# Moving scaled norms, an up projection and an out projection at the end of windowed attention

## The chip, the cores and the metric

The kernel runs on one core of a Trainium2 chip. The core has five engines that run their own instruction streams and meet at semaphores: TensorE (PE, matmuls and transposes; its weight loads are listed as PEld), VectorE (DVE), ScalarE (ACT), GpSimd (POOL) and SyncE (SP, which issues DMAs). The metric is the device time of one execution in microseconds; three executions before the change gave 2340.21, 2340.26 and 2348.76, median 2340.26.

## The reference

Input x is 4 batches of 1024 tokens by 256 features. First comes causal attention with 16 heads of 16, which this change does not touch. Then a stack of two layers of windowed attention and feed-forward; B, N there are 4 and 1024, 8 heads of 64, windows of 128, HID = 682:

```python
def _layer(x, wqkv, qs, ksc, wo, lg, lb, w1, b1, w2, b2):
    h = shift_token(x)                    # second half of the features from the token before
    q, k, v = split(h @ wqkv); q, k = l2norm(q) * qs, l2norm(k) * ksc
    q, k = rotary_xpos(q, k)
    o = local_attention(q, k, v)          # each window sees itself and the one before
    x = x + o @ wo
    h = shift_token(x)
    h = (h - mean) / sqrt(var + 1e-05) * lg + lb
    a, g = split(h @ w1 + b1)
    return x + (a * gelu(g)) @ w2 + b2
```

The result is x + stack(layernorm(x)), after the first attention's residual.

## The kernel before

`layers` does the two layers, four batches each: eight passes of attention(it) and feed_forward(it), written out one after the other in each engine's stream. What stands in a stream is done in that order; an instruction starts when those ahead of it on its engine are through and its semaphores have the values it waits for. `Count.of(it, i)` is the value after item i of pass it (negative i: items of the pass before).

Attention goes through 32 units (UNITS), each a couple of heads of one window of 128 tokens, four units a window. For unit u PE makes scores into one of the score banks s0 and s1 (L1382, two units at a time), DVE masks them and takes the maximum (L1894), ACT takes the exponential (L1628), PE turns the probabilities in pt_ps (L1448, two units behind), ACT copies them out (L1644), and PE multiplies by the values into o_ps (L1473). For each window the sums of probabilities are inverted, widened by ACT (L1653), spread over the features by PE in turn_ps (L1457); ACT copies o_ps to o_t (L1660) and DVE scales o_t (L1951). When the last units are in work, no new scores follow, and this chain over PE, ACT and DVE has little beside it.

The out projection (L1395) works on halves of 512 tokens: half c, feature block m. The half c = 0 and its norm are done inside attention, beside later windows: out projection, residual sum (DVE, L1904), turn to tokens first (PE, L1403), statistics and normalising (DVE, L1913, L1924), turn back (PE, L1412), scaled norms (`scale_norm`, ACT, L1636: four ACTIVATEs, a full and a rounded copy of two feature blocks) and the low part (`split_norm`, DVE, L1930). scale_norm stands at unit NORM_AT + 6 = 30 of ACT's loop, split_norm at NORM_AT + 7 of DVE's. These steps use two of the three banks of qkv_ps, as ln_ps.

The feed-forward has six up projections (L1435) for each half, each of 12 matmuls into a couple of banks (the last, of 42 features, 6 matmuls into one bank): s0 and s1, or pt_ps and o_ps, in turn (`up_pair`). Behind each: GELU (ACT, L1691), gate product (DVE, L1986, counts hidden_ready), rounding (ACT, L1699), low part (DVE, L1992, counts hidden_split). Up projection i waits for the gate product of i - 2, which frees its banks. The down projection (L1516, 18 matmuls for each feature block) follows, and the next pass's query, key and value projections (L1336) stand between. The first up projection is in the attention loop, at u = UNITS; the out projection of the second half follows it. At the end of the feed-forward the next pass's first scores (L1382) go into s0 and s1.

A float32 matmul (not a transpose, nor one of the rounded float32r kind) appears in the traces as two records, so the out projection's 8 matmuls are "x16" there.

Of the kernel before, what the change touches and what calls it, by code (L numbers as in the profile page):

```python
# [22 lines left out]
P = 128  # L23
# [1061 lines left out]
def layers(nc, ident, neg_half, passed, a):  # L1085
# [5 lines left out]
    with ExitStack() as ctx:  # L1091
# [11 lines left out]
        up_pair = lambda c, j: pair[(c + j) % 2]  # L1103
# [213 lines left out]
        def _(pe):  # L1317
# [48 lines left out]
            def scores(it, g):  # L1366
                w = 2 * g // PAIRS
                pe.wait_ge(turn_copied.sem, turn_copied.of(it, 2 * w + 1))
                pe.wait_ge(s_masked.sem, s_masked.of(it, 4 * g - 1))
                if g == 0:  # L1370
                    pe.wait_ge(hidden_ready.sem, hidden_ready.of(it, -1))
                first, last = max(0, w - 1), w
                if first % KR < last % KR:
                    runs = [(first, last + 1)]
                else:
                    runs = [(t, t + 1) for t in range(first, last + 1)]
                for h, (t0, t1) in itertools.product(range(2), runs):
                    for u in (2 * g, 2 * g + 1):
                        p, side = place(u, h)
                        r = slice(side * HD2, (side + 1) * HD2)  # L1380
                        to = (h + 1) * PW - (w + 1 - t0) * P
                        mm = pe.matmul(s_ps[side][:, to:to + (t1 - t0) * P], q_t[r, w % 2, p, :],  # L1382
                                       k_t[r, p, t0 % KR * P:(t0 % KR + t1 - t0) * P], start=True, stop=True)
                        if h and t1 == w + 1:
                            mm.then_inc(s_ready.sem, 1)

            def project_out(it, c, m):
# [3 lines left out]
                if c == 1 and m == 0:  # L1391
                    pe.wait_ge(hn_t_ready.sem, hn_t_ready.of(it, KD - 1))
                pe.wait_ge(o_scaled.sem, o_scaled.of(it, (c + 1) * WPC - 1))
                for k in range(INNER // P):
                    mm = pe.matmul(ln_ps[m], w_out[:, k, m * P:(m + 1) * P],  # L1395
                                   o_t[:, k, :], start=k == 0, stop=k == INNER // P - 1)
                mm.then_inc(wo_ready.sem, 1)

            def tokens_first(it, c):
                pe.wait_ge(mid_ready.sem, mid_ready.of(it, (c + 1) * KD - 1))  # L1400
                for t in range(TC):
# [14 lines left out]
            def up(it, c, j):  # L1416
                i = c * HT + j
                pe.wait_ge(hn_t_split.sem, hn_t_split.of(it, (c + 1) * KD - 1))
                if i == 0:
                    pe.wait_ge(s_masked.sem, s_masked.of(it, 2 * UNITS - 1))  # L1420
                elif i == 1:
                    pe.wait_ge(pt_copied.sem, pt_copied.of(it, UNITS - 1))
                    pe.wait_ge(o_copied.sem, o_copied.of(it, NT - 1))
                elif i == HT:
                    pe.wait_ge(hidden_ready.sem, hidden_ready.of(it, i - 1))
                elif i == HT + 1:
                    pe.wait_ge(out_ready.sem, out_ready.of(it, KD - 1))
                elif i > 1:
                    pe.wait_ge(hidden_ready.sem, hidden_ready.of(it, i - 2))
# [9 lines left out]
            def attention(it):  # L1439
# [39 lines left out]
                for u in range(UNITS + 3):  # L1479
# [22 lines left out]
                    if u == UNITS:  # L1502
                        up(it, 0, 0)
# [3 lines left out]
            def feed_forward(it, more):  # L1507
                def down(c, m):
# [3 lines left out]
                    for n, (j, w, h) in enumerate(steps):  # L1512
# [3 lines left out]
                        mm = pe.matmul(pair[c][m][:, :], w_down(w, j, m)[0:rows], hidden[0:rows, h, j, :],  # L1516
# [16 lines left out]
                up(it, 0, 1)  # L1533
                tokens_first(it, 1)
                for j in range(2, HT):
# [46 lines left out]
        def _(act):  # L1582
# [56 lines left out]
            def attention(it):  # L1639
# [23 lines left out]
                for u in range(UNITS + 3):  # L1663
# [17 lines left out]
                    if u == NORM_AT + 6:  # L1681
                        scale_norm(it, 0)
# [160 lines left out]
        def _(dve):  # L1843
# [54 lines left out]
            def residual(it, c, m):  # L1898
# [5 lines left out]
                dve.tensor_tensor(x_mid[:, m, s], ln_ps[m], x_in[:, m, s], ALU.add).then_inc(mid_ready.sem, 1)  # L1904
# [35 lines left out]
            def attention(it):  # L1940
# [13 lines left out]
                for u in range(UNITS + 4):  # L1954
# [23 lines left out]
                    if u == NORM_AT + 7:  # L1978
                        split_norm(it, 0)

            def feed_forward(it, more):
# [13 lines left out]
                def output(c, m):  # L1995
                    dve.wait_ge(down_ready.sem, down_ready.of(it, c * KD + m))
                    s = slice(m + c * CH, m + (c + 1) * CH)
                    dve.scalar_tensor_tensor(out=x_mid[:, m, s], in0=pair[c][m][:, :], scalar=b_down[:, m:m + 1],
# [4 lines left out]
                for j in range(HT):  # L2003
# [3 lines left out]
                    if j == 1:  # L2007
# [146 lines left out]
```

## Time and profile before

| | us |
|---|---|
| median of three executions | 2340.26 |
| the profiled execution | 2343.61 |
| its span | 2341.9 |
| PE, DVE, ACT, POOL busy | 86%, 62%, 53%, 34% |
| mean granted clock of PE | 0.951 |

The eight passes fill the span from about 900 us on; a pass of the timeline takes some 180 us. Busy time is the time in which an engine has an instruction in work; a granted clock of 1.00 is the full level of PE's clock. In timelines a row merges neighbouring instructions of one kind; the bracket tells how long the engine stood idle before it, and which instruction ended the wait.

### The profile page before, as it was taken

The page shows a single profiled execution, that of the slowest core. Times are in us where ns is not written, and L with a number is a line of the kernel's source. Part 1 is how long each engine was busy: PE and PEld are TensorE (multiplying, and loading weights), DVE is VectorE, ACT ScalarE, POOL GpSimd, SP SyncE. Part 2 cuts the span into 40 slices and gives each one's busy share as a digit, 9 for nine tenths or more (in the row PEclk, how much of TensorE's full clock was granted, in tenths as well). Part 3 has the DMA queues.
Part 4 walks back from the last instruction along what each step waited for, and adds up shares of the span by engine and source line. Part 5 has one row for each costly group of instructions (what it writes and reads, how often), then busy time and mean ns, then how long its engine had stood idle before and what let it go on. Part 6 is the DMA issues. An engine that isn't in the chain of part 4 may idle for free.

```text
span 2341.9 us, 36128 instructions
## 1 busy us (share of the span) xinstructions
PE 2007.6 (86%) x11968; PEld 1252.2 (53%) x11968; DVE 1458.2 (62%) x3942; ACT 1243.1 (53%) x2980; POOL 798.4 (34%) x663
## 2 busy tenths in 40 slices
PE   5566899999987727999989989989989989989988
PEld 3232233333332525666666666656667667657656
DVE  5467788888873435646646646755745745746744
ACT  1121666666666315735745754753754754754663
POOL 2233322111231336415405505515604613613620
PEclk9896899999999868999999999999999999999999
DMA  5646844555620631000000000012100000000000
GB/s 146 151 131 137 148 96 70 78 82 82 108 93 20 168 119 77 1 27 10 1 28 10 1 24 14 1 66 85 29 19 19 19 19 18 19 13 25 19 1 27
DMA packets 124455, 128.97 MB, mean 55 GB/s; under 512 B 50460, under 2 KB 101232, under 8 KB 123248
## 3 DMA queue, kind: packets, MB, share of 16 engines
q1 hardware_dynamic: 123696, 117.75, 21.7%
q0 software_dynamic: 576, 8.91, 1.0%
q8 instruction: 98, 1.61, 0.3%
q14 instruction: 85, 0.70, 0.1%
HBM read 75.51 MB, written 50.86 MB: 54 GB/s over the span
## 4 chain that ended last, share of the span: by engine, by line
PE 35%; DVE 12%; ACT 8%; issue 6%; POOL 2%; DMA 0%; DVEq 0%; SPq 0%; POOLq 0%; ACTq 0%
DVE rot_s L1885 5%; PE qkv_ps L1395 5%; PE s_ps L1435 4%; PE qkv_ps L1336 4%; PE s_ps L1382 3%; PE s_ps L1516 3%; PE pt_ps L1448 3%; PE o_ps L1473 3%; DVE p_sb L1894 3%; ACT p_sb L1628 3%; POOL inv_norm L1779 2%; PE pt_ps L1435 2%; PE o_ps L1435 2%; PE pt_ps L1516 2%; PE o_ps L1516 2%
## 5 line engine op out<-in xcount | busy, mean ns | idle before, releaser
L717 ACT ACTIVATE probs<-st_ps 128x512 f32<-128x512 f32 (+3 forms) x768 | 330.1, 494 | 170.1 <-PE st_ps L625 169.8
L1336 PE MATMUL qkv_ps<-w_qkv,x_parts 128*128 128x512 f32 x1152 | 307.2, 410 | 33.9 <-DVE x_parts L1859 24.6
L1628 ACT ACTIVATE p_sb<-p_sb,negmax 128x256 f32<-128x256 f32 (+1 forms) x512 | 249.5, 490 | 72.8 <-DVE negmax L1894 72.7
L610 PE MATMUL s_ps<-k_stack,q_stack 96*128 96x512 bf16 (+3 forms) x768 | 243.7, 349 | 40.9 <-DVE piece_negmax L762 25.4
L762 DVE CUSTOM_DVE_ANT_0 seen<-s_ps,causal 128x128 f32<-128x128 f32 (+3 forms) x512 | 233.8, 484 | 45.8 <-PE s_ps L610 45.5
L625 PE MATMUL st_ps<-q_stack,k_stack 98*128 98x512 bf16 (+3 forms) x768 | 243.0, 337 | 14.5 <-ACT probs L717 10.1
L1336 PEld LDWEIGHTS qkv_ps<-w_qkv,x_parts 128*128 128x128 f32 x1152 | 210.8, 193 | 80.9 <-issue 39.7
L1894 DVE CUSTOM_DVE_ANT_0 p_sb<-s_ps,band 128x256 f32<-128x256 f32 (+1 forms) x512 | 185.4, 401 | 88.2 <-PE s_ps L1382 84.5
L1644 ACT COPY p_t<-pt_ps 128x512 f32<-128x512 f32 (+1 forms) x256 | 143.5, 561 | 160.7 <-PE pt_ps L1448 159.4
L1787 POOL TENSOR_TENSOR rot_c<-qn,turn_by 128x512 f32<-128x512 f32 x128 | 178.5, 1414 | 137.5 <-PE turn_ps L1362 111.6
L844 POOL TENSOR_SCALAR_AFFINE_SELECT probs<-probs 128x512 f32<-128x512 f32 x128 | 81.6, 637 | 419.1 <-ACT probs L717 419.1
L1885 DVE TENSOR_TENSOR rot_s<-qn,turn_by 128x256 f32<-128x256 f32 x256 | 202.9, 852 | 0.3
L765 DVE TENSOR_REDUCE piece_negmax<-s_ps 128x1 f32<-128x512 f32 x256 | 176.0, 687 | 30.1 <-PE s_ps L610 29.6
L1779 POOL TENSOR_TENSOR inv_norm<-sum_sq,neg_half 128x16 f32<-128x16 f32 x64 | 187.6, 2931 | 5.3
L1448 PE MATMUL pt_ps<-ident,p_sb 128*128 128x128 f32 x960 | 163.8, 291 | 26.9 <-ACT p_t L1644 26.9
L1792 POOL TENSOR_TENSOR rot_c<-rot_c,rot_s 128x1024 f32<-128x1024 f32 x64 | 158.5, 2476 | 60.2 <-DVE rot_s L1885 60.2
L1382 PE MATMUL s_ps<-k_t,q_t 64*128 64x256 f32 (+1 forms) x1152 | 139.1, 363 | 39.3 <-DVE negmax L1894 30.2
L639 PE MATMUL o_ps<-probs,v_sb 128*32 128x512 f32 (+3 forms) x1536 | 166.5, 506 | 1.2 <-POOL probs L844 0.7
L625 PEld LDWEIGHTS st_ps<-q_stack,k_stack 98*128 98x128 bf16 x768 | 72.4, 98 | 162.4 <-ACT probs L717 124.3
L610 PEld LDWEIGHTS s_ps<-k_stack,q_stack 96*128 96x128 bf16 x768 | 76.2, 100 | 154.5 <-DVE piece_negmax L762 71.7
L1448 PEld LDWEIGHTS pt_ps<-ident,p_sb 128*128 128x128 f32 x960 | 102.7, 142 | 85.3 <-issue 75.8
L1865 DVE TENSOR_REDUCE sum_sq<-squares 128x16 f32<-128x1024 f32 x64 | 77.9, 1217 | 109.9 <-ACT squares L1591 109.9
(146 smaller groups left out, 3512.0 us busy)
## 6 DMA issues: line engine op xcount, KB each, us to landing
qk_scratch<-parts SPq DMA_DIRECT2D x64, 192.0 KB, 2.8
q_stack<-qk_scratch SPq DMA_DIRECT2D x96, 128.0 KB, 6.8
k_stack<-qk_scratch SPq DMA_DIRECT2D x96, 128.0 KB, 7.1
w_ffn<-ffn_weights POOLq DMA_DIRECT2D x4, 2176.0 KB, 11.5
v_scratch<-v_out SPq DMA_DIRECT2D x32, 256.0 KB, 2.6
v_sb<-v_scratch SPq DMA_DIRECT2D x16, 512.0 KB, 10.3
x_in<-xt_scratch SPq DMA_DIRECT2D x16, 512.0 KB, 4.1
ffn_weights<-w_high SPq DMA_DIRECT2D x2, 2176.0 KB, 8.0
```

Source lines behind the costliest of these rows:

```text
L610: pe.matmul(s_ps[i % 3][:, 0:kw], q_stack[0:STK, slot, h, qt * P:(qt + 1) * P], k_stack[0:STK, slot, h, k0:k0 + kw], start=True, stop=True ...
L625: pe.matmul(st_ps[i % 3][:, q0:CH], k_stack[0:STK + SHIFT, slot, h, kt * P:(kt + 1) * P], q_stack[0:STK + SHIFT, slot, h, c * CH + q0:(c + ...
L717: act.activation(probs[:, n % 3, h, q0:CH], st_ps[i % 3][:, q0:CH], ACT.Exp).then_inc(exp_done.sem, 1)
L762: dve.tensor_tensor_reduce(seen[:, i % 3, 0:kw], s_ps[i % 3][:, 0:kw], causal[:, CH - kw:CH], -1.0, BIG, ALU.add, ALU.min, result).then_in ...
L1336: mm = pe.matmul(qkv_ps[:, part * CH:(part + 1) * CH], x_parts[:, w % XR, xp, k, :], w_qkv[:, wp, k, part * INNER:(part + 1) * INNER], sta ...
L1382: mm = pe.matmul(s_ps[side][:, to:to + (t1 - t0) * P], q_t[r, w % 2, p, :], k_t[r, p, t0 % KR * P:(t0 % KR + t1 - t0) * P], start=True, st ...
L1435: mm = pe.matmul(up_pair(c, j)[bank][0:rows, :], w_up(w, k, tile)[:, 0:rows], hn_t[:, h, k, :], start=n == 0, stop=n == len(steps) - 1)
L1448: mm = pe.transpose(pt_ps[:, (h * 2 + kt) * P:(h * 2 + kt + 1) * P], p_sb[:, u % 4, h, kt * P:(kt + 1) * P], ident[:, :])
L1628: act.activation(p_sb[:, u % 4, h, k0:PW], p_sb[:, u % 4, h, k0:PW], ACT.Exp, scale=-1.0, bias=negmax[:, u % 4, h:h + 1], accum_out=total[ ...
L1779: pool.tensor_tensor(inv_norm[:, :], sum_sq[:, 1, :], neg_half[:, 0:2 * H2], ALU.pow)\
L1885: dve.tensor_tensor(dst[:, :, o], src[:, :, i], turn_by[:, w, 2 * j + 1, o].unsqueeze(1) .to_broadcast([P, H2, half]), ALU.mult).then_inc( ...
L1894: dve.tensor_tensor_reduce(p_sb[:, u % 4, h, k0:PW], s_ps[u % 2][:, h * PW + k0:(h + 1) * PW], band[:, k0:PW], 1.0, BIG, ALU.add, ALU.min, ...
```

## The change

It is in `layers` alone. (1) The out projection of the second half writes s0 and s1 (`out_bank`) and waits for the last masks and not for the norms of the first half. (2) scale_norm and split_norm of the first half stand behind the attention loops of ACT and DVE. (3) The first up projection stands behind the out projection. (4) Up projections start with the couple pt_ps and o_ps (`up_pair` turned by one), and the down projections take the banks that `down_bank` names. (5) The first scores of the next pass wait for the gate product before the last. (6) The statistics of the second half stand behind the first gate product.

```diff
--- before.py
+++ after.py
@@ -1100,7 +1100,9 @@
 
         pair = ((s0, s1), (pt_ps, o_ps))
-        up_pair = lambda c, j: pair[(c + j) % 2]
+        up_pair = lambda c, j: pair[(c + j + 1) % 2]
+        down_bank = lambda c, m: pair[1][m if c == 0 else 1 - m]
+        out_bank = lambda c, m: ln_ps[m] if c == 0 else s_ps[m]
 
@@ -1368,7 +1370,7 @@
                 pe.wait_ge(s_masked.sem, s_masked.of(it, 4 * g - 1))
                 if g == 0:
-                    pe.wait_ge(hidden_ready.sem, hidden_ready.of(it, -1))
+                    pe.wait_ge(hidden_ready.sem, hidden_ready.of(it, -2))
                 first, last = max(0, w - 1), w
@@ -1389,15 +1391,17 @@
                     pe.wait_ge(qn_ready.sem, qn_ready.of(it, NT - 1))
                 if c == 1 and m == 0:
-                    pe.wait_ge(hn_t_ready.sem, hn_t_ready.of(it, KD - 1))
+                    pe.wait_ge(s_masked.sem, s_masked.of(it, 2 * UNITS - 1))
                 pe.wait_ge(o_scaled.sem, o_scaled.of(it, (c + 1) * WPC - 1))
                 for k in range(INNER // P):
-                    mm = pe.matmul(ln_ps[m], w_out[:, k, m * P:(m + 1) * P],
+                    mm = pe.matmul(out_bank(c, m)[:, :], w_out[:, k, m * P:(m + 1) * P],
                                    o_t[:, k, :], start=k == 0, stop=k == INNER // P - 1)
...
             def tokens_first(it, c):
                 pe.wait_ge(mid_ready.sem, mid_ready.of(it, (c + 1) * KD - 1))
+                if c == 1:
+                    pe.wait_ge(hn_t_ready.sem, hn_t_ready.of(it, KD - 1))
                 for t in range(TC):
@@ -1417,10 +1421,10 @@
                 pe.wait_ge(hn_t_split.sem, hn_t_split.of(it, (c + 1) * KD - 1))
                 if i == 0:
-                    pe.wait_ge(s_masked.sem, s_masked.of(it, 2 * UNITS - 1))
-                elif i == 1:
                     pe.wait_ge(pt_copied.sem, pt_copied.of(it, UNITS - 1))
                     pe.wait_ge(o_copied.sem, o_copied.of(it, NT - 1))
+                elif i == 1:
+                    pe.wait_ge(mid_ready.sem, mid_ready.of(it, NC * KD - 1))
                 elif i == HT:
@@ -1499,8 +1503,6 @@
                     if u == NORM_AT + 5:
                         features_first(it, 0)
-                    if u == UNITS:
-                        up(it, 0, 0)
                     if u >= 4 and u % 2 == 0:
@@ -1513,7 +1515,7 @@
                         if n == (HT - 1) * len(PARTS):
                             pe.wait_ge(hidden_split.sem, hidden_split.of(it, (c + 1) * HT - 1))
-                        mm = pe.matmul(pair[c][m][:, :], w_down(w, j, m)[0:rows], hidden[0:rows, h, j, :],
+                        mm = pe.matmul(down_bank(c, m)[:, :], w_down(w, j, m)[0:rows], hidden[0:rows, h, j, :],
                                        start=n == 0, stop=n == len(steps) - 1)
@@ -1530,9 +1532,9 @@
                 project_out(it, 1, 0)
                 project_out(it, 1, 1)
-                up(it, 0, 1)
+                up(it, 0, 0)
                 tokens_first(it, 1)
-                for j in range(2, HT):
+                for j in range(1, HT):
                     up(it, 0, j)
@@ -1678,8 +1680,7 @@
                     if u >= PAIRS + 2 and (u - 2) % PAIRS == 0:
                         copy_output((u - 2) // PAIRS - 1)
-                    if u == NORM_AT + 6:
-                        scale_norm(it, 0)
+                scale_norm(it, 0)
 
@@ -1901,7 +1902,7 @@
                         dve.wait_ge(stored, it * (16 * NC) + 16)
                 s = slice(m + c * CH, m + (c + 1) * CH)
-                dve.tensor_tensor(x_mid[:, m, s], ln_ps[m], x_in[:, m, s], ALU.add).then_inc(mid_ready.sem, 1)
+                dve.tensor_tensor(x_mid[:, m, s], out_bank(c, m)[:, :], x_in[:, m, s], ALU.add).then_inc(mid_ready.sem, 1)
 
@@ -1975,8 +1976,7 @@
                     if u in (NORM_AT + 3, NORM_AT + 4):
                         normalise(it, 0, u - NORM_AT - 3)
-                    if u == NORM_AT + 7:
-                        split_norm(it, 0)
+                split_norm(it, 0)
 
@@ -1995,7 +1995,7 @@
                     dve.wait_ge(down_ready.sem, down_ready.of(it, c * KD + m))
                     s = slice(m + c * CH, m + (c + 1) * CH)
-                    dve.scalar_tensor_tensor(out=x_mid[:, m, s], in0=pair[c][m][:, :], scalar=b_down[:, m:m + 1],
+                    dve.scalar_tensor_tensor(out=x_mid[:, m, s], in0=down_bank(c, m)[:, :], scalar=b_down[:, m:m + 1],
                                              in1=x_mid[:, m, s], op0=ALU.add, op1=ALU.add).then_inc(out_ready.sem, 1)
@@ -2004,7 +2004,7 @@
                         low(0, j - 1)
                     gated(0, j)
-                    if j == 1:
+                    if j == 0:
                         statistics(it, 1, 0)
...
```

PE, end of attention and start of the feed-forward, before. Names: pt_ps<-p_sb is a turn of probabilities, o_ps<-p_t values, turn_ps<-inv_wide the spread of sums, <-o_t the out projection, <-hn_t an up projection.

```order
L1473 MATMUL o_ps<-p_t,v_tok 64x128 x8
L1448 MATMUL pt_ps<-ident,p_sb 128x128 x8
L1435 MATMUL s_ps<-hn_t,w_ffn 128x512 x12
L1473 MATMUL o_ps<-p_t,v_tok 64x128 x8
L1448 MATMUL pt_ps<-ident,p_sb 128x128 x4
L1457 MATMUL turn_ps<-ident,inv_wide 128x128 x4
L1473 MATMUL o_ps<-p_t,v_tok 64x128 x8
L1395 MATMUL qkv_ps<-o_t,w_out 128x512 x8
L1435 MATMUL pt_ps<-hn_t,w_ffn 128x512 x6
L1435 MATMUL o_ps<-hn_t,w_ffn 128x512 x6
L1403 MATMUL qkv_ps<-ident,x_mid 128x128 x8
L1435 MATMUL s_ps<-hn_t,w_ffn 128x512 x12
```

And after:

```order
L1477 MATMUL o_ps<-p_t,v_tok 64x128 x8
L1452 MATMUL pt_ps<-ident,p_sb 128x128 x8
L1477 MATMUL o_ps<-p_t,v_tok 64x128 x8
L1452 MATMUL pt_ps<-ident,p_sb 128x128 x4
L1461 MATMUL turn_ps<-ident,inv_wide 128x128 x4
L1477 MATMUL o_ps<-p_t,v_tok 64x128 x8
L1397 MATMUL s_ps<-o_t,w_out 128x512 x8
L1439 MATMUL pt_ps<-hn_t,w_ffn 128x512 x6
L1439 MATMUL o_ps<-hn_t,w_ffn 128x512 x6
L1407 MATMUL qkv_ps<-ident,x_mid 128x128 x8
L1439 MATMUL s_ps<-hn_t,w_ffn 128x512 x12
L1439 MATMUL pt_ps<-hn_t,w_ffn 128x512 x6
```

The 12 matmuls into s_ps between the turns and the values are gone; their work, now into pt_ps and o_ps, follows the out projection, which has moved into s_ps.

ACT at the same place, before (p_t<-pt_ps is the copy of turned probabilities, hn and hn_t the scaled norms, o_t<-o_ps the copy of outputs, gate GELU):

```order
L1660 COPY o_t<-o_ps 128x4x128 [waits pv_done2]
L1636 ACTIVATE hn<-qkv_ps,ln_b,ln_g 128x512 [waits back_ready]
L1636 ACTIVATE hn_t<-qkv_ps,ln_b,ln_g 128x512
L1636 ACTIVATE hn<-qkv_ps,ln_b,ln_g 128x512
L1636 ACTIVATE hn_t<-qkv_ps,ln_b,ln_g 128x512
L1644 COPY p_t<-pt_ps 128x512 [waits pv_done2,pt_ready]
L1628 ACTIVATE p_sb,total<-p_sb,negmax 128x256 [waits s_masked] x2
L1644 COPY p_t<-pt_ps 128x512 [waits pv_done2,pt_ready] x2
L1653 COPY inv_wide<-inv_total 128x512 [waits spread,inv_sum]
L1660 COPY o_t<-o_ps 128x4x128 [waits pv_done2]
L1691 ACT_TABLE_LOAD [waits hidden_split]
L1691 ACTIVATE gate<-s_ps,b_up 128x512 [waits up_ready]
```

And after:

```order
L1662 COPY o_t<-o_ps 128x4x128 [waits pv_done2]
L1646 COPY p_t<-pt_ps 128x512 [waits pv_done2,pt_ready]
L1630 ACTIVATE p_sb,total<-p_sb,negmax 128x256 [waits s_masked] x2
L1646 COPY p_t<-pt_ps 128x512 [waits pv_done2,pt_ready] x2
L1655 COPY inv_wide<-inv_total 128x512 [waits spread,inv_sum]
L1662 COPY o_t<-o_ps 128x4x128 [waits pv_done2]
L1638 ACTIVATE hn<-qkv_ps,ln_b,ln_g 128x512 [waits back_ready]
L1638 ACTIVATE hn_t<-qkv_ps,ln_b,ln_g 128x512
L1638 ACTIVATE hn<-qkv_ps,ln_b,ln_g 128x512
L1638 ACTIVATE hn_t<-qkv_ps,ln_b,ln_g 128x512
L1692 ACT_TABLE_LOAD [waits hidden_split]
L1692 ACTIVATE gate<-o_ps,b_up 128x512 [waits up_ready]
```

The four scaled norms went from ahead of the copies for the last three units to behind the last copy of outputs. The table load stands behind them and waits for hidden_split, the GELU behind it for up_ready.

## Rows read from the trace of the kernel before

**Rows 1.** Page, part 1: engine, busy us, share of the span, instructions.
```profile
PE 2007.6 (86%) x11968; PEld 1252.2 (53%) x11968; DVE 1458.2 (62%) x3942; ACT 1243.1 (53%) x2980; POOL 798.4 (34%) x663
```

**Rows 2.** Waits of PE, 900 to 2342 us: waiting line, releaser: total, times, longest.
```profile
PE s_ps L1382 <- DVE negmax L1894: 30.2, 32, 2.1
PE pt_ps L1448 <- ACT p_t L1644: 26.9, 8, 3.4
...
PE turn_ps L1457 <- ACT inv_wide L1653: 14.1, 16, 1.2
PE qkv_ps L1395 <- DVE o_t L1951: 12.6, 8, 1.6
PE s_ps L1516 <- DVE hidden L1992: 8.2, 8, 3.5
PE s_ps L1382 <- DVE gate L1986: 7.9, 7, 1.2
```

**Rows 3.** Timeline of PE, second pass: start, duration, line, output<-inputs, [idle before].
```profile
1175.16 0.66 PE L1448 MATMUL pt_ps<-ident,p_sb 128*128 128x128 f32 x4
1179.17 1.09 PE L1448 MATMUL pt_ps<-ident,p_sb 128*128 128x128 f32 x4 [3.36 <-ACT p_t L1644]
1179.91 5.16 PE L1435 MATMUL s_ps<-hn_t,w_ffn 128*128 128x512 f32 x12
...
1186.03 0.66 PE L1448 MATMUL pt_ps<-ident,p_sb 128*128 128x128 f32 x4
1187.88 0.66 PE L1457 MATMUL turn_ps<-ident,inv_wide 128*128 128x128 f32 x4 [1.19 <-ACT inv_wide L1653]
...
1191.13 7.11 PE L1395 MATMUL qkv_ps<-o_t,w_out 128*128 128x512 f32 x16 [1.57 <-DVE o_t L1951]
```

**Rows 4.** Timeline of ACT, the same stretch.
```profile
1175.76 0.79 ACT L1636 ACTIVATE hn<-qkv_ps,ln_b,ln_g 128x512 f32<-128x512 f32 x1
...
1178.42 0.61 ACT L1644 COPY p_t<-pt_ps 128x512 f32<-128x512 f32 x1
1178.89 0.55 ACT L1628 ACTIVATE p_sb<-p_sb,negmax 128x256 f32<-128x256 f32 x1
...
1190.21 1.28 ACT L1691 ACT_TABLE_LOAD   x1
1191.50 0.69 ACT L1691 ACTIVATE gate<-s_ps,b_up 128x512 f32<-128x512 f32 x1
```

**Rows 5.** Windows, one a pass: length, busy of the engines, PE's clock, DMA, GB/s.
```profile
994.24:1009.86 15.62, 9.50 (x58) 7.12 (x57) 2.97 (x5) 7.40 (x15) 0.00 (x0) 0.78 0.01 2
...
1357.05:1369.89 12.84, 6.72 (x58) 5.15 (x57) 2.97 (x5) 7.30 (x15) 0.00 (x0) 1.00 0.00 0
...
sum 115.39, PE 66.41 PEld 51.02 DVE 23.77 ACT 59.00 POOL 0.00; mean PE 8.30 PEld 6.38 DVE 2.97 ACT 7.37 POOL 0.00
```

**Rows 6.** Timeline of PE, third pass, the first up projection.
```profile
1360.41 0.63 PE L1448 MATMUL pt_ps<-ident,p_sb 128*128 128x128 f32 x4 [3.36 <-ACT p_t L1644]
1360.80 3.03 PE L1435 MATMUL s_ps<-hn_t,w_ffn 128*128 128x512 f32 x12
```

**Rows 7.** Timeline of DVE, second pass, first gate product and statistics.
```profile
1198.88 0.74 DVE L1986 SCALAR_TENSOR_TENSOR gate<-s_ps,b_up,gate 128x512 f32<-128x512 f32 x1
...
1202.44 1.42 DVE L1913 BATCH_NORM_STATS2 stats<-qkv_ps 128x6 f32<-128x256 f32 x4
1204.00 0.38 DVE L1917 BATCH_NORM_AGGREGATE mean_var<-stats 128x2 f32<-128x6 f32 x4
```

**Rows 8.** Timelines of PE, then of DVE, second pass, first scores of the next.
```profile
1252.84 0.71 PE L1382 MATMUL s_ps<-k_t,q_t 64*128 64x128 f32 x8 [1.05 <-DVE gate L1986]
...
1258.06 4.65 PE L1516 MATMUL o_ps<-hidden,w_ffn 128*128 128x512 f32 x18
...
1253.38 1.43 DVE L1992 TENSOR_TENSOR hidden<-gate,hidden 42x512 fp32r<-42x512 f32 x1 [0.69 <-ACT hidden L1699]
```

**Rows 9.** Timeline of POOL, second pass.
```profile
1256.90 2.93 POOL L1779 TENSOR_TENSOR inv_norm<-sum_sq,neg_half 128x16 f32<-128x16 f32 x1
```

## The prediction

> **What bounds the kernel now.** I read the page first. TensorE (PE) is busy for 86% of the span and every other engine for less [rows 1]: PE is the engine whose idle stretches are worth looking for, though busy for 86% does not make each of its waits cost time. The second view is the list of waits of PE over the windowed-attention layers [rows 2]. The largest one, 30.2 us for the scores behind the masked maxima, is spread over 32 places and untouched by the change. Five stand around the change: 8 waits of at most 3.4 us for a copy of turned probabilities (26.9 us), the sums' 16 waits for the widened copy (14.1 us), 8 before the second out projection (12.6 us), 8 before the down projection (8.2 us) and 7 of the first scores of the next batch for a gate product (7.9 us). A count of 7 or 8 says: once in each of the eight passes.
>
> The third view is PE's timeline at one pass's end of attention [rows 3]. The probabilities of unit 29 are turned until 1175.82 (1175.16 and 0.66); then PE idles 3.36 us. The timeline of ScalarE (ACT) says why [rows 4]: from 1175.76 on it makes the four scaled norms of the first half, and only at 1178.42 the copy that PE waits for. Then PE turns unit 30, does the first up projection (12 matmuls, 1179.91), values, and the turn of unit 31, waits 1.19 and 1.57 us through the serial end (copy, widen, spread, values, copy, scale) and starts the second out projection at 1191.13. A wait here is on the path that sets the end: behind it the list names no wait of PE before that of the down projection [rows 2], so all that follows moves with it.
>
> The fourth view is a table of windows, one for each pass, from the end of unit 29's turn to the start of the out projection [rows 5]: 115.39 us in all eight. They are not alike: 15.62 us at a granted clock of 0.78 in the first, 12.84 at 1.00 in the third, with the same number of matmuls. So the two levels are 1.2 and 2.4 GHz here, and in seven of the eight passes the idle stretch was followed by work at the lower one: in the first timeline the 12 up matmuls take 5.16 us. At full clock the eight would take 8 x 12.84 = 102.72, so the low clock costs 115.39 - 102.72 = 12.67 us.
>
> **The change part by part.** *The four scaled norms behind the attention loop (ACT).* They held ACT from 1175.76, where the first of the four starts, to 1178.42, 2.66 us [rows 4]. Without them the copy of unit 29 starts as soon as its turn has ended (1175.82), takes its 0.6, and PE's 3.36 wait shrinks by the 2.66, less 0.02 of hand-over: to about 0.72. Where do they go? Behind the last copy of attention outputs, where the table load stands now: 1190.21, 0.92 us ahead of the out projection [rows 3, 4]. So they run under the out projection's 7.1 us and end 1.8 us into it, and VectorE's second subtraction of 0.7 follows. The first up projection, which needs them, stands behind the out projection: 4 us of room. Cost 0. If that cover were gone, they would cost 2.66 + 0.7 for each pass.
>
> *The first up projection out of the attention tail (PE).* 12 matmuls. In the third pass they lie between the turn's end at 1361.04 and their own at 1363.83 [rows 6]: 2.80 us at full clock; the difference to the 5.16 above is in the clock term. So the tail gets 2.80 shorter in front of the out projection, and 2.80 longer behind it. It is neutral by itself. It filled no wait: it delayed unit 31's turn, on which the serial end hangs.
>
> *The tail, added up again from its links,* as a test of the two: turn of unit 30 starts 0.75 after 1175.82 and takes 0.6; values 1.03; turn of unit 31 0.6 (from the up projection's end at 1185.07 to 1186.69 in rows 3, 1.62 for both); then from 1186.70 to 1191.13 as before, 4.43. Sum 7.40. By subtraction from the full-clock pass: 12.84 - 2.64 - 2.80 = 7.40. ACT's exponentials of unit 31 start 0.47 after the copy of unit 29 [rows 4]; two of about 0.5 each end 1.5 us after that unit's turn, and the turn of unit 31 is due at 2.4, so they add nothing. Per pass the stretch to the same place behind the first up projection is 7.40 + 2.80 = 10.20, in eight 81.6. Saved: 115.39 - 81.6 = 33.8 us, of it 8 x 2.64 = 21.1 for the wait and 12.7 for the clock.
>
> *Whether the clock falls in the new tail.* What is left of idle is 0.72, 1.19 and 1.57 us with short turns between. In the third pass the last two (and even the 3.36) stand in a window of clock 1.00 [rows 5]. I take full clock, bounded below by no loss and above by the loss before, 12.7.
>
> *Out projection into the score banks.* 8 matmuls, as before. The banks' last readers are the masks of unit 31, whose result the exponentials at 1178.89 use without a wait [rows 4], so the new wait passes at once. The turn of tokens (L1403) keeps its wait for the residual sums and gets one for the norms; the first up projection's 2.8 us now stand between out projection and it and hide the second sum (0.7). Cost 0.
>
> *Statistics one step earlier (VectorE).* They followed the second gate product, 1202.44 to 1204.38 [rows 7], and now follow the first. PE needs the second gate product before its fourth up projection. Behind the first one it has the token turn (8 small matmuls; four take 0.66, rows 3, so about 1) and two up projections, 1 + 5.6 us. The second gate product comes after the second up projection (1 + 2.8), GELU 0.69 and gate 0.74, at 5.3 with hand-overs; VectorE itself is free of the first gate product (1.5), statistics (1.94) and a low part (0.7) at 4.2. Room 1.3 us, cost 0.
>
> *GELU's table load.* It took 1.28 us in the gap before the first GELU [rows 4]. The order of instructions shows it waiting for hidden_split alone, with up_ready on the ACTIVATE behind it, so it runs right behind the norms, still under the out projection. Cost 0; were it to start behind the up projection, the first gate product would come 1.28 + 1.5 = 2.8 us after it, and the third up projection starts at 3.8. The Trainium skill, ScalarE: Activation LUTs, What ACT_TABLE_LOAD costs, gives 2.66 us for a switch, 1283 ns of load and 1380 of drain. The row has the load's 1.28, and the GELU starts 1.29 us after the load does, so no drain is seen there. By the page's sum, and with the load exposed, the first gate product comes at 4.2 and each pass loses 0.4 us, 3 in all.
>
> *Bank couples turned by one.* Up and down projections take the other couple; sizes and order stay. The one gain is at the end: the last, narrow up projection now lies in pt_ps and not in a score bank, so the next batch's first scores wait for the fifth gate product and not the sixth. That removes the seven waits of 7.9 us [rows 2]. Does it arrive? The scores move from 1252.84 to 1251.79 [rows 8]; the two down projections behind them follow. Their last three matmuls wait for the last low part, done at 1254.8, while the first would reach them near 1256. The second ends at 1261.7 instead of 1262.7, and what hangs on it next (residual, unit vectors) also needs POOL's inverse norms, done at 1259.8 [rows 9]: 2 us of room. So all of it arrives; bounds 0 and 7.9, I take 7.9.
>
> *Sum.* 33.8 + 7.9 = 41.7 us. The profiled execution took 2343.61 us (span 2341.9), so 2301.9; the median of the runs before is 2340.26, 3.35 lower, which gives 2298.6: 2299 us.
>
> **The rivals.** *The clock falls in the new tail as it did in the old.* For it: seven of eight passes did. Against: the wait it followed is cut to a fifth. Then 12.7 is lost again: 2311. The worst form, the out projection at half rate for as long as in the first pass, costs 15.62 - 12.84 = 2.8 in each of eight, 22: 2321. The Trainium skill, TensorE: Matmul & The Clock Gate, HAM oscillation, tells of kernels that fall back at each recurring wait and start each piece of work cold; that rule would ask for this rival. The rows agree for the 3.36 wait, in seven passes of eight, and do not for the 1.19 and 1.57.
>
> *The first scores' gain is given back*, because VectorE's chain at that point (rotation, low part until 1254.8) decides and not PE: 41.7 - 7.9, 2306. Against: the 2 us of room above.
>
> *The tail does not shrink*: the exponentials or maxima of the last units are late next and PE waits for them as long. Then 21.1 of the sum goes, and the clock's 12.7 with it: only 7.9 left, 2332. Against: the exponentials of unit 31 follow their copy with no wait, even at 1178.89 [rows 4], and PE's wait names the copy alone.
>
> *Slower: PE and the gate chain fall into lock-step.* If the up projections behind the first had to wait for the gate product of the one just before (GELU 0.69, gate 0.74, 1.48 with hand-overs) and not of the one before that, five steps of eight passes would lose 5 x 1.48 x 8 = 59; less 41.7, it ends at 2358. It decides from 41.7 / 40 = 1.04 us per step on. For it: statistics now stand ahead of the second gate product, and the first norms no longer run long before. Against: 1.3 us or more of room at each step above.
>
> **How the numbers follow.** The forecast has 0.66, with a range of its own of 2293 to 2306 (single links off by 0.1 us move 0.8 us each, the level of the runs by 2 or 3). The clock rival has 0.14, the lost scores 0.09, the tail that does not shrink 0.06, lock-step 0.03; 0.02 is left for what I do not see. The range goes up to 2316, to take in the clock rival's 2311 and the lost scores; down to 2291, for a faster level of runs and for low clock at the start of attention that may fall away. A measurement of this kernel tells 0.5%, 11.7 us, from no change: faster means under 2328.6. The first three cases are faster, the fourth lies within, lock-step is slower; of the unseen 0.02 half goes to each of the first two: 0.90, 0.07, 0.03.
>
> **What would show it.** In the profile of the changed kernel PE's wait for the copy of turned probabilities falls from 3.4 to 0.7 us, the one before the out projection stays at 1.57 in eight, and unit 29's turn to out projection takes 7.4 us at a clock of 1.00. The four norms stand on ACT under the out projection, with the table load behind them. The first up projection starts with the out projection's end, with no wait, and 12 of its matmuls take 2.8 us. The scores' wait for the gate product is gone. I would be wrong if the out projection runs at half clock, if up projections two to six wait, or if the wait before the down projection (0.66) grows by more than the tail gives.

## The result and the profile after

| | before | after |
|---|---|---|
| median | 2344.42 us (4 runs, 2340.21 to 2348.76) | 2299.92 us (4 runs, 2298.03 to 2306.98) |
| ratio | | 0.9826, 95% interval 0.9807 to 0.9844 |
| profiled execution (span, mean clock) | 2343.61 (2341.9, 0.951) | 2298.97 (2296.1, 0.960) |
| first matmul of the windowed layers | 856.9 | 851.5 |
| from there to the end of the span | 1485.0 | 1444.7 |

The kernel is faster; 2299 us had been forecast. The fourth execution of the kernel before moved its median from 2340.26, from which the forecast was worked out, to 2344.42. The last row is the measure used below: 40.3 us less. I call this time *the layers' stretch*. It repeats better than the whole: it was 1484.8 and 1444.1 in second profiles of the two kernels, while the start of the layers came at 852.6 and 851.5.

Part 1 of the page after:

```profile
PE 1990.5 (87%) x11968; PEld 1241.2 (54%) x11968; DVE 1457.9 (63%) x3942; ACT 1243.2 (54%) x2980; POOL 798.9 (35%) x663
```

Against [rows 1] PE's busy time is 17.1 us less with the same instructions, since less of its work runs at half clock. The rest of the gain is idle time. Its list of waits, 900 to 2300 us, says which:

```profile
PE s_ps L1384 <- DVE negmax L1895: 29.9, 32, 2.1
...
PE turn_ps L1461 <- ACT inv_wide L1655: 14.0, 16, 1.2
PE s_ps L1397 <- DVE o_t L1952: 12.6, 8, 1.6
PE pt_ps L1518 <- DVE hidden L1992: 8.1, 8, 3.5
PE pt_ps L1452 <- ACT p_t L1646: 6.1, 8, 0.8
```

The 26.9 us for the copy p_t in [rows 2] are 6.1, and the first scores' 7.9 for the gate product have no row any more. The other waits of [rows 2] stand as they were; no new one took the place of those removed.

PE's timeline at the same end of attention as [rows 3], second pass:

```profile
1164.34 0.66 PE L1452 MATMUL pt_ps<-ident,p_sb 128*128 128x128 f32 x4
1165.76 0.63 PE L1452 MATMUL pt_ps<-ident,p_sb 128*128 128x128 f32 x4 [0.77 <-ACT p_t L1646]
1166.32 1.09 PE L1477 MATMUL o_ps<-p_t,v_tok 128*64 128x128 f32 x16
1167.35 0.66 PE L1452 MATMUL pt_ps<-ident,p_sb 128*128 128x128 f32 x4
1169.20 0.66 PE L1461 MATMUL turn_ps<-ident,inv_wide 128*128 128x128 f32 x4 [1.19 <-ACT inv_wide L1655]
1169.78 1.09 PE L1477 MATMUL o_ps<-p_t,v_tok 128*64 128x128 f32 x16
1172.45 7.11 PE L1397 MATMUL s_ps<-o_t,w_out 128*128 128x512 f32 x16 [1.57 <-DVE o_t L1952]
1178.99 1.96 PE L1439 MATMUL pt_ps<-hn_t,w_ffn 128*128 128x512 f32 x6
1180.79 1.54 PE L1439 MATMUL o_ps<-hn_t,w_ffn 128*128 128x512 f32 x6
```

Unit 29's turn ends at 1165.00, the out projection starts at 1172.45: 7.45 us instead of the 15.31 there. The up projection (two groups of six here, one for each bank) follows the out projection without a wait.

The windows over this tail, one a pass, as in [rows 5]:

```profile
989.91:997.37 7.46, 3.93 (x46) 2.99 (x45) 1.58 (x3) 4.72 (x12) 0.00 (x0) 1.00 0.00 1
...
sum 59.62, PE 31.38 PEld 23.93 DVE 12.69 ACT 37.72 POOL 0.00; mean PE 3.92 PEld 2.99 DVE 1.59 ACT 4.71 POOL 0.00
```

59.6 us against 115.4, and 8 x 2.80 = 22.4 of the difference is the up projection, which now stands behind. The clock is 1.00 in all eight.

ACT's timeline, second pass, answers to [rows 4]:

```profile
1171.40 0.78 ACT L1638 ACTIVATE hn<-qkv_ps,ln_b,ln_g 128x512 f32<-128x512 f32 x1
...
1173.40 0.79 ACT L1638 ACTIVATE hn_t<-qkv_ps,ln_b,ln_g 128x512 fp32r<-128x512 f32 x1
1174.22 1.28 ACT L1692 ACT_TABLE_LOAD   x1
1182.37 0.69 ACT L1692 ACTIVATE gate<-o_ps,b_up 128x512 f32<-128x512 f32 x1 [6.87 <-PE o_ps L1439]
```

The norms start 1.05 us ahead of the out projection (1171.40 against 1172.45) and run on under it, as priced, with the table load right behind them and 8 us ahead of the GELU. DVE's subtraction that the up projection needs, and its statistics behind the first gate product ([rows 7] were behind the second):

```profile
1174.23 0.69 DVE L1931 TENSOR_TENSOR hn_t<-hn,hn_t 128x512 fp32r<-128x512 f32 x1 [0.65 <-ACT hn_t L1638]
...
1183.09 0.75 DVE L1986 SCALAR_TENSOR_TENSOR gate<-pt_ps,b_up,gate 128x512 f32<-128x512 f32 x1 [2.81 <-ACT gate L1692]
1183.76 1.42 DVE L1914 BATCH_NORM_STATS2 stats<-qkv_ps 128x6 f32<-128x256 f32 x4
...
1186.75 0.75 DVE L1986 SCALAR_TENSOR_TENSOR gate<-s_ps,b_up,gate 128x512 f32<-128x512 f32 x1 [0.48 <-ACT gate L1692]
```

The subtraction ends at 1174.92, 4.1 us before the up projection. The second gate product ends at 1187.50; the fourth up projection starts at 1188.62 in the same timeline of PE, so 1.1 us of room are left where the prediction had 1.3.

### The profile page after: what moved, and what is told of

Its sections match the earlier page's. It is cut to its first block, busy times and chain, and to the rows that moved or that the text cites. A ratio compares the mean times of both kernels' runs of the same rounds, so it can differ in the third digit from the quotient of the medians.

```text
span 2296.1 us, 36136 instructions
## 1 busy us (share of the span) xinstructions
PE 1990.5 (87%) x11968; PEld 1241.2 (54%) x11968; DVE 1457.9 (63%) x3942; ACT 1243.2 (54%) x2980; POOL 798.9 (35%) x663
## 4 chain that ended last, share of the span: by engine, by line
PE 38%; DVE 10%; ACT 8%; issue 5%; POOL 2%; DMA 0%; DVEq 0%; SPq 0%; ACTq 0%; POOLq 0%
PE qkv_ps L1338 5%; PE s_ps L1439 4%; DVE rot_s L1886 4%; PE s_ps L1384 4%; PE pt_ps L1518 3%; PE o_ps L1518 3%; PE pt_ps L1452 3%; PE o_ps L1477 3%; ACT p_sb L1630 3%; DVE p_sb L1895 3%; PE s_ps L1397 2%; PE qkv_ps L1397 2%; PE pt_ps L1439 2%; PE o_ps L1439 2%; POOL inv_norm L1780 2%
## 5 line engine op out<-in xcount | busy, mean ns | idle before, releaser
L625 PE MATMUL st_ps<-q_stack,k_stack 98*128 98x512 bf16 (+3 forms) x768 | 240.8, 334 | 14.4 <-ACT probs L717 10.1
```

Of the source, the lines that this page charges most:

```text
L625: pe.matmul(st_ps[i % 3][:, q0:CH], k_stack[0:STK + SHIFT, slot, h, kt * P:(kt + 1) * P], q_stack[0:STK + SHIFT, slot, h, c * CH + q0:(c + ...
```

## The experiments

Three groups of kernels were run; in each, the kernel before ran on the same chip (medians 2340.87 for the first four kernels, 2337.72 for the next four, 2338.21 for the last four). "Stretch" is that of the profiled execution.

| kernel | median us (runs) | ratio to before, 95% | stretch |
|---|---|---|---|
| norms_back | 2345.60 (10) | 1.0034 [1.0013, 1.0054] | 1486.5 |
| scores_wait_back | 2306.93 (4) | 0.9858 [0.9836, 0.9881] | 1453.8 |
| before_fill | 2330.70 (8) | 0.9960 [0.9943, 0.9978] | 1473.0 |
| out_in_norm_banks | 2329.74 (10) | 0.9954 [0.9941, 0.9968] | 1472.9 |
| out_split | 2277.87 (4) | 0.9741 [0.9717, 0.9764] | 1424.2 |
| after_again | 2296.14 (4) | 0.9822 [0.9795, 0.9849] | 1444.1 |
| stats_back | 2308.38 (4) | 0.9868 [0.9842, 0.9894] | 1450.0 |
| norms_plus3 | 2301.71 (4) | 0.9841 [0.9816, 0.9866] | 1443.1 |
| norms_back_fill | 2319.83 (4) | 0.9916 [0.9888, 0.9945] | 1463.2 |
| norms_plus7 | 2333.56 (10) | 0.9974 [0.9958, 0.9991] | 1476.1 |
| stats_again | 2305.72 (1) | | 1448.5 |
| before_again | 2340.29 (1) | | 1484.8 |

**norms_back**: of the kernel after, the norms alone go back into the loop.

```diff
-                scale_norm(it, 0)
+                    if u == NORM_AT + 6:
+                        scale_norm(it, 0)
...
-                split_norm(it, 0)
+                    if u == NORM_AT + 7:
+                        split_norm(it, 0)
```

> The changed kernel with one thing undone: the four scaled norms and the low part of the first half stand in the attention loop again, at their old units. My theory: PE's wait ahead of unit 30's turn goes back from 0.77 to 3.4 us (+21 us in eight), and the idle stretch brings the lower clock back in most passes (up to +12.7), so 2321 to 2336, likeliest 2334, that is the kernel before less the 7.9 us of the first scores. If the gain came from the up projection's place instead, this run stays near 2300.

The whole gain is gone, more than expected: the median lies 10 us above the range, and 0.1 to 0.5% above the kernel before. PE's timeline in the first pass:

```profile
991.17 0.66 PE L1452 MATMUL pt_ps<-ident,p_sb 128*128 128x128 f32 x4
995.18 1.08 PE L1452 MATMUL pt_ps<-ident,p_sb 128*128 128x128 f32 x4 [3.36 <-ACT p_t L1646]
996.20 1.98 PE L1477 MATMUL o_ps<-p_t,v_tok 128*64 128x128 f32 x16
998.11 1.12 PE L1452 MATMUL pt_ps<-ident,p_sb 128*128 128x128 f32 x4
1000.41 1.11 PE L1461 MATMUL turn_ps<-ident,inv_wide 128*128 128x128 f32 x4 [1.19 <-ACT inv_wide L1655]
1001.46 1.98 PE L1477 MATMUL o_ps<-p_t,v_tok 128*64 128x128 f32 x16
1005.01 8.71 PE L1397 MATMUL s_ps<-o_t,w_out 128*128 128x512 f32 x16 [1.57 <-DVE o_t L1953]
```

The 3.36 us wait is back, and behind it everything runs at half rate until some way into the out projection (turns 1.1 instead of 0.6, values 1.98 instead of 1.09, the out projection 8.71 instead of 7.11). The norms' place decides wait and clock together. The next runs separate them.

**scores_wait_back**: the turned bank couples stay, and the first scores wait for the last gate product again.

```diff
-                    pe.wait_ge(hidden_ready.sem, hidden_ready.of(it, -2))
+                    pe.wait_ge(hidden_ready.sem, hidden_ready.of(it, -1))
```

> The changed kernel, with the first scores of the next pass waiting for the last gate product again. My theory: seven waits of about 1.1 us come back and each reaches the end, 2300 + 7.9 = 2308. The rival (VectorE's chain decides there): the waits come back in the list but the time stays at 2300.

Its list of waits has the old row back, and the stretch is 9.1 us longer:

```profile
PE s_ps L1384 <- DVE gate L1986: 7.9, 7, 1.2
```

All of this wait's removal arrives at the end; the rival in which it is given back falls. (Where the other 1.2 us lie is told below.)

**before_fill**: the kernel before, with three matmuls for no use (into the values' projection bank) where PE would idle before unit 30's turn.

```diff
+                def keep_busy():
+                    pe.wait_ge(v_copied.sem, v_copied.of(it, NT - 1))
+                    for n in range(3):
+                        mm = pe.matmul(v_ps, ident[:, :], w_out[:, 0:2, :].rearrange("p k n -> p (k n)"),
+                                       start=True, stop=True)
...
+                    if u == UNITS:
+                        keep_busy()
```

> The kernel before, with three matmuls of 0.86 us more (512 columns, into the idle value bank, their product used by nobody) between the turns of units 29 and 30, where PE idles 3.36 us. They fit into the wait, so they cost nothing, and keep PE at work. My theory of the clock term: the granted clock stays 1.00 in all eight passes and the kernel is 12.7 us faster than before, some 2331. The rival (the low clock there hides in other waits and costs nothing): no change.

PE's timeline in the first pass, and a window from inside the fill to the out projection:

```profile
988.87 0.66 PE L1454 MATMUL pt_ps<-ident,p_sb 128*128 128x128 f32 x4
989.36 2.74 PE L1443 MATMUL qkv_ps<-w_out,ident 128*128 128x512 f32 x6
992.88 0.63 PE L1454 MATMUL pt_ps<-ident,p_sb 128*128 128x128 f32 x4 [0.78 <-ACT p_t L1652]
993.26 3.03 PE L1435 MATMUL s_ps<-hn_t,w_ffn 128*128 128x512 f32 x12
...
1002.35 7.10 PE L1395 MATMUL qkv_ps<-o_t,w_out 128*128 128x512 f32 x16 [1.57 <-DVE o_t L1959]
```

```profile
990.52:1002.35 11.83, 8.29 (x60) 5.52 (x59) 2.28 (x4) 6.29 (x13) 0.00 (x0) 1.00 0.00 1
```

The turn of unit 30 is no earlier (it starts 3.35 us after unit 29's ends at 989.53; the fill takes the wait's place), yet the up projection takes 3.03 us and not the 5.46 of this pass before, and the clock is 1.00. From the end of unit 29's turn to the out projection it is 12.82 us, as in the full-clock pass of [rows 5], and not 15.62. The stretch is 12.0 us shorter; the medians differ by 10.2. This is the clock term alone, and it is the idle PE that costs it.

**norms_back_fill**: norms_back with the same three matmuls.

> The changed kernel with the norms back in the attention loop and, as in the kernel before with filling, three matmuls of 0.86 us whose product nobody uses in PE's wait. Norms_back alone cost 42 us of the stretch from the first matmul of the windowed layers to the end, with the clock at half for longer than before. My theory: with the clock held at full, 8 x 2.64 = 21 us are left, so the stretch is 1444.7 + 21 = 1466 and the time about 2319; the same number follows from the kernel before with filling (1473.0) less the 7.9 us of the first scores, 1465, if the place of the first up projection is neutral at full clock. If its place is worth something of its own, the two sums part.

1463.2, 2 to 3 us below the two sums expected. At full clock the norms in the loop cost 1463.2 - 1444.7 = 18.5 us. And norms_back minus this one, 23.3 us (25.8 by the medians), is the clock's share there: about twice the 12.0 of the kernel before, from the same 3.36 us of idle.

**out_in_norm_banks**: the whole change except its first part; the second out projection goes into the banks of the norms, as before, and so waits until the norms are read.

```diff
-        out_bank = lambda c, m: ln_ps[m] if c == 0 else s_ps[m]
+        out_bank = lambda c, m: ln_ps[m]
...
                 if c == 1 and m == 0:
-                    pe.wait_ge(s_masked.sem, s_masked.of(it, 2 * UNITS - 1))
+                    pe.wait_ge(hn_t_ready.sem, hn_t_ready.of(it, KD - 1))
...
```

> The changed kernel with the second out projection in the norm banks again, so that it has to wait for the scaled norms, which now stand behind the last copy. My theory: its wait grows from 1.57 to about 3.3 us (+14 in eight), and the longer idle brings the lower clock to the out projection in most passes (up to +12 more): 2314 to 2328. If the banks do not matter: 2300.

```profile
PE qkv_ps L1397 <- ACT hn_t L1639: 27.0, 8, 3.4
...
PE pt_ps L1453 <- ACT p_t L1647: 6.1, 8, 0.8
```

The wait for the turned copy is short, but 3.4 us stand before the out projection in each pass instead of 1.57: 14.4 us in eight. The stretch is 28.2 longer than after; the other 13.8 go with the clock (first pass: the same 16 out-projection matmuls took 8.83 and not 7.11). The median is 1.7 us above the expected range. So the score banks are what lets the norms move.

**norms_plus3** and **norms_plus7**: after, with three or seven unused activations of 1.03 us ahead of the norms.

```diff
...
+                if c == 0:
+                    act.wait_ge(summed.sem, summed.of(it, NT - 1))
+                    for extra in range(3):
+                        act.activation(squares[:, :], q_ps, ACT.Square).then_inc(spared, 1)
+                        act.wait_ge(spared, 3 * it + extra + 1)
```

> The changed kernel with three wide ACTIVATEs (1.0 us each, their result used by nobody) ahead of the four scaled norms of the first half. In the changed kernel's trace the low parts are done 4.6 us before the first up projection starts. So 3.3 us more should be covered by the out projection: no change, 2300. If the norms had no room, +26.

> The changed kernel with seven wide ACTIVATEs (1.05 us each as measured with three, their result used by nobody) ahead of the four scaled norms of the first half: 7.3 us more, 2.7 more than the 4.6 us of room. My theory: the first up projection waits 2.7 us in each pass, 22 in all, and may start at the lower clock, up to 12 more: 2318 to 2330. If the norms were covered by more than the out projection: 2300.

Three move nothing (1443.1). Seven bring a new wait of PE, at the size expected:

```profile
PE pt_ps L1440 <- DVE hn_t L1937: 22.5, 8, 2.8
```

The stretch grows by 31.4, 22.5 of waits and 8.9 beyond them. The room under the out projection is shown from both sides: three of them (3.1 us) fit, and seven, which held ACT for 7.36 us in the second pass, brought 2.8 us of wait, so it is about 4.6 us by this run and 4.1 by the rows of after. In five of the eight passes the granted clock between the first half's out projection and the third up projection was 0.97, against 1.00 in all eight after: a wait of 2.8 us can cost the clock too. The median is 3.6 us above the range, whose upper end held the clock; the profiled execution, 2328.61 us, lies in it.

**stats_back** and **stats_again** (the same kernel): statistics behind the second gate product, where they were.

```diff
-                    if j == 0:
+                    if j == 1:
                         statistics(it, 1, 0)
```

> The changed kernel with the statistics of the second half behind the second gate product again. My theory: no change within 1 us, PE waits at none of the six up projections either way; it could lose a few us if the turn to features first, and with it the down projection, then waits for the normalised tiles.

> The changed kernel with the statistics behind the second gate product, once more: its windowed layers started at 860.5 us in its profile, those of the changed kernel at 851.4. If that is the execution's chance, the start moves now; from the first matmul of the windowed layers to the end it should take 1450 again.

What I expected was wrong: the stretch is 1450.0 and 1448.5 against 1444.7 and 1444.1, 5.3 and 4.4 us longer. Two rows of the list of waits grew:

```profile
PE pt_ps L1518 <- DVE hidden L1992: 9.9, 9, 3.6
...
PE s_ps L1439 <- DVE gate L1986: 1.9, 8, 0.5
```

These two are 3.7 us of it (8.1 and nothing in the kernel after). My reading, which no run isolates: with the up projections started later against VectorE's chain, the old place delays gate products and then the last low part before the down projection. The rest of the profiled execution's longer time (2312.24 us) is the start of the layers, below.

**after_again** and **before_again** repeat the two kernels.

> The changed kernel once more, on the chip of the runs beside it: 2300.

> The kernel before once more, to see whether the start of its windowed layers (856.9 us) and the stretch behind it (1485.0 us) repeat.

The ratio came again (0.9822; 41.6 us). The start of the layers did not:

```profile
856.89 5.27 PE L1336 MATMUL qkv_ps<-w_qkv,x_parts 128*128 128x512 f32 x15 [24.55 <-DVE x_parts L1859]
```

```profile
852.59 5.87 PE L1336 MATMUL qkv_ps<-w_qkv,x_parts 128*128 128x512 f32 x18 [25.15 <-DVE x_parts L1859]
```

These are two executions of the kernel before. It was 860.5 for stats_back and 855.5 for stats_again, which are one kernel, 851.5 both times for after, and 850.7 for before_fill. The work ahead of this point is the same in all of them.

**out_split**: after, with the part of the out projection that is ready early drawn into the waits of the serial end. The windows 4 to 6 of the second half are complete before the last one, so their 384 columns of the first output block go in two pieces, ahead of the spread sums and behind the last values.

```diff
+            early = 3 * P
+            def project_early(it, k0):
+                if k0 == 0:
+                    pe.wait_ge(s_masked.sem, s_masked.of(it, 2 * UNITS - 1))
+                    pe.wait_ge(o_scaled.sem, o_scaled.of(it, NT - 2))
+                for k in (k0, k0 + 1):
+                    pe.matmul(s_ps[0][:, 0:early], w_out[:, k, 0:P], o_t[:, k, 0:early],
+                              start=k == 0, stop=k == INNER // P - 1)
...
+                    if u == UNITS + 2:
+                        project_early(it, 0)
...
+                project_early(it, 2)
                 project_out(it, 1, 0)
```

> The changed kernel, with the first feature block of the second out projection cut at window 7: for the first three windows (384 columns), two of its four accumulation steps go into PE's 1.19 us wait for the widened copy and two into the 1.57 us wait before the out projection; its last window and the second block follow as before. From 2 x 3.55 us behind the last scaling, 3.55 + about 0.8 are left. The first filling takes 1.33 us and delays the chain by 0.15 to 0.3. My theory (PE's time behind the tail sets the end): 2.4 to 2.7 us less in each pass, 19 to 22 in all, 2279. Rival: the norms or the gate chain are late next and take it back, 2290 to 2300.

PE's timeline, first pass:

```profile
997.39 0.66 PE L1463 MATMUL pt_ps<-ident,p_sb 128*128 128x128 f32 x4
997.89 1.46 PE L1396 MATMUL s_ps<-o_t,w_out 128*128 128x384 f32 x4
999.24 0.66 PE L1472 MATMUL turn_ps<-ident,inv_wide 128*128 128x128 f32 x4
999.83 1.09 PE L1488 MATMUL o_ps<-p_t,v_tok 128*64 128x128 f32 x16
1000.85 1.56 PE L1396 MATMUL s_ps<-o_t,w_out 128*128 128x384 f32 x4
1002.50 4.57 PE L1408 MATMUL s_ps<-o_t,w_out 128*128 128x128 f32 x16
```

The waits of 1.19 and 1.57 us are gone at this place and the stretch is 20.5 us shorter than after. At 2277.87 us this version beats both kernels.

## Why the prediction was right

*The sum.* 41.7 us were forecast; the layers' stretch gives 40.3 and, from the second profiles, 40.7. The runs closed it by parts: norms 18.5 (norms_back_fill), clock 12.0 (before_fill), first scores 9.1 (scores_wait_back), together 39.6. The prediction had 21.1, 12.7 and 7.9. The timelines say where each part lies. Cut each pass at two matmuls that every kernel has: the first of the first half's out projection, and the first of the third up projection. The tail and all that the change moves around it lie between the two. The rest of the stretch is a piece ahead of the first pass's mark, seven pieces from one pass to the next, in which the first scores stand, and one behind the last pass.

| kernel | between the two marks, eight passes | the rest | of it, the seven pieces |
|---|---|---|---|
| before | 426.8 | 1058.2 | 895.5 |
| before_fill | 414.1 | 1058.9 | 894.8 |
| norms_back_fill | 414.7 | 1048.5 | 885.2 |
| norms_back | 436.4 | 1050.2 | 886.6 |
| scores_wait_back | 393.9 | 1059.8 | 895.6 |
| after | 393.9 | 1050.7 | 887.0 |

There the clock is 426.8 - 414.1 = 12.7 us, as forecast, and the norms 414.7 - 393.9 = 20.8, against 21.1. The first scores are 895.6 - 887.0 = 8.6 in the seven pieces, against 7.9. The piece ahead of the first mark, which the change leaves alone, was 108.9 us before and 110.1 after; over all profiles it lay between 108.6 and 110.8. So the three terms held within 1 us each. Their sum, 42.1, less 0.6 for the up projection's place (414.7 against 414.1) and 1.1 for that piece, is the stretch's 40.3 within 0.1. That the median after came within 1 us of 2299 is luck in part: the medians of this comparison differ by 44.5 us, those of the next by 41.6, and the four executions of either kernel spread over 8.6 and 9.0 us. What lies beyond the stretch (44.6 us between the two profiled executions) is the start of the layers, 5.4 us earlier in one than in the other, which varies as much between two executions of one kernel.

*The norms.* Each wait shrank from 3.36 to 0.77 us, 2.59 where 2.64 was priced, or 20.8 in the rows of waits, and 20.8 arrived in the table. The tail of 7.40 us was 7.46. The difference of stretches, 18.5, is 2.3 smaller because the kernel after was slower elsewhere in its profile, mostly by the clock: in the pieces between its first three passes the granted clock was 0.99 and each took 125.8 us, in norms_back_fill 1.00 and 125.5. Why it fell there in one and not in the other is open.

*Costs of nothing.* Norms, table load and out projection in the score banks: none shows a wait, and norms_plus3 and norms_plus7 bound the room. The first scores gave 9.1 us by the stretch, 1.2 more than the wait's 7.9: 0.55 of that lies ahead of the first pass's out projection, where the changed wait does not stand, and 8.6 are left for the seven passes.

*The up projection's place, "neutral by itself".* True at full clock: 414.1 us between the two marks in before_fill and 414.7 in norms_back_fill, which differ in this place. Not true at a fallen clock: there the up projection behind the wait was the dense work after which the clock was full again, and without it the clock cost 436.4 - 414.7 = 21.7 us instead of 12.7. It is not so in every pass: against the 51.8 us of full clock, the first three passes of norms_back lost 4.7, 3.4 and 5.1 us (2.8, 2.5 and 0 before), the fourth and fifth 1.4 and 1.3 (1.5 and 1.3 before), and the seventh nothing. The prediction's "neutral by itself" missed this; it cost nothing only because the wait went too. It is why norms_back lay above what I had expected.

*Statistics one step earlier, "cost 0".* The move cost nothing, but it is no free choice: left out, it would have lost 4 to 5 us. The room of 1.3 us was worked out for the new place alone, and the old place was never priced in the new order.

*The rivals.* The clock stayed at 1.00 over the 0.77, 1.19 and 1.57 us that are left; the tail shrank; the scores' gain arrived; the gate chain fell into no lock-step. norms_plus7 and out_in_norm_banks show that the first rival was near: where a wait of 2.8 or 3.4 us returns, the loss is larger than the waits by 8.9 and 13.8 us.

## What to carry to other kernels

Where a serial end over several engines is the wait, take out of every engine's stream what does not belong to it, ScalarE's as much as TensorE's, and put it under the next dense matmul; the free bank that lets the matmul start first is the key. Price an idle stretch of TensorE with the clock behind it, and ask what work follows: in most passes here dense work ended the loss early and short turns made it last. Then cut the next matmul into the parts whose inputs are ready, and put them into the waits that are left.

## What the runs showed of the hardware

The same idle stretch of 3.36 us cost 12.7 us through the clock in eight passes where 12 wide matmuls (128x512) followed one short turn later (before against before_fill), and 21.7 where only turns and values came until the out projection (norms_back against norms_back_fill), with 0 to 5.1 us in a single pass. Filling it with three matmuls that compute nothing of use took these costs away. The granted clock fell behind 3.36 us of idle in seven of eight passes of the kernel before, of norms_back and (3.37 us, ahead of the out projection) of out_in_norm_banks, behind 2.8 us in five of eight (norms_plus7), and behind 0.77, 1.19 and 1.57 us in none of the eight passes after. The layers started between 850.7 and 860.5 us with identical work ahead of them, so differences of a few us between kernels are read from a stretch behind it.
